# Cross attention with row turns one slot later, a spread prologue, and plain fp32 projections in the first layer

## The reference, cut to what matters

```python
x = cross_attn(layernorm(x, ln2_g, ln2_b), context, q2_w, k2_w, v2_w, o2_w, o2_b) + x
...
q = linear(x, qw).reshape(Bq, Nq, H, DH)
k = linear(ctx, kw).reshape(Bq, Nk, H, DH)
v = linear(ctx, vw).reshape(Bq, Nk, H, DH)
sim = jnp.einsum('bihd,bjhd->bhij', q, k) * scale
attn = jax.nn.softmax(sim, axis=-1)
out = jnp.einsum('bhij,bjhd->bihd', attn, v).reshape(Bq, Nq, D)
return linear(out, ow, ob)
```

## Time and profile before

| | |
|---|---|
| median of three runs | 4440.8 us (4432.99 to 4448.74) |
| the profiled execution | 4438.94 us, its span 4437.1 us |
| mean granted clock of TensorE | 0.935 of full |
| busy over the span: TensorE, VectorE, ScalarE, POOL | 90%, 68%, 41%, 41% |
| narrow cross attention | first DMA at 1042.66, first score 1091.37, next stage 1414.97 |
| wide cross attention | first DMA at 3607.91, first score 3626.93 |

### The profile page before, as it was taken

The page is one execution under the profiler, slowest core; times in us unless marked ns, Lnnn a source line. Parts: engine busy times, 40 slices in busy tenths (PEclk is TensorE's granted clock), DMA queues, the critical chain, the costliest instruction groups (busy, mean ns, idle before and its releaser), DMA issues. The chain is left out here.

```text
span 4437.1 us, 66504 instructions
## 1 busy us (share of the span) xinstructions
PE 4009.9 (90%) x25111; PEld 2704.9 (61%) x25111; DVE 3034.0 (68%) x4959; ACT 1797.1 (41%) x2646; POOL 1814.9 (41%) x1175
## 2 busy tenths in 40 slices
PE   0779999995877997998999999999999979999899
PEld 0633434432665776776666666666666647777687
DVE  6779999973776655776666766676666646656565
ACT  0227777773444333111333333333333333434332
POOL 0158800001333110001677877877787752212200
PEclk9869999996788998999999999999999978989999
DMA  4554534212342101777121211211112010000100
GB/s 120 169 87 72 62 38 49 35 18 54 59 72 48 43 11 33 268 277 271 49 72 49 71 50 49 72 49 60 61 49 72 25 38 1 10 10 1 35 15 20
DMA packets 311705, 293.29 MB, mean 66 GB/s; under 512 B 132684, under 2 KB 233612, under 8 KB 311140
## 3 DMA queue, kind: packets, MB, share of 16 engines
q1 hardware_dynamic: 309476, 282.53, 24.9%
q0 software_dynamic: 1920, 6.61, 0.5%
HBM read 160.74 MB, written 127.28 MB: 65 GB/s over the span
## 5 line engine op out<-in xcount | busy, mean ns | idle before, releaser
L1702 POOL TENSOR_TENSOR f_sums<-f_sums,f_probs 128x1024 f32<-128x1024 f32 x384 | 915.6, 2384 | 154.6 <-ACT f_probs L1821 116.9
L1719 DVE TENSOR_REDUCE f_mx<-f_s 128x1 f32<-128x512 f32 x1024 | 659.8, 686 | 374.9 <-PE f_s L1844 363.7
L1821 ACT ACTIVATE f_probs<-f_st 128x1024 f32<-128x1024 f32 x512 | 525.0, 1027 | 932.2 <-PE f_st L1867 927.4
L1331 DVE TENSOR_REDUCE f_mx<-f_s 128x1 f32<-128x512 f32 x1024 | 638.7, 683 | 50.0 <-PE f_s L1462 27.9
L1442 ACT ACTIVATE f_probs<-f_st 128x512 f32<-128x512 f32 x1024 | 536.0, 600 | 208.2 <-PE f_st L1479 207.8
L1844 PE MATMUL f_s<-f_k,f_q 64*128 64x512 f32 x3072 | 508.0, 409 | 20.4 <-DMA f_k<-k 13.5
L1867 PE MATMUL f_st<-f_q,f_k 64*128 64x512 f32 x3072 | 485.2, 390 | 1.1 <-ACT f_probs L1821 1.0
L1881 PE MATMUL f_acc<-f_probs,f_v 128*64 128x512 f32 x2048 | 466.5, 597 | 0.0
L1844 PEld LDWEIGHTS f_s<-f_k,f_q 64*128 64x128 f32 x3072 | 339.0, 186 | 163.9 <-issue 113.1
L2313 POOL TENSOR_TENSOR f_probs<-f_probs,f_rden 128x616 f32<-128x616 f32 x128 | 161.4, 1261 | 556.0 <-DVE f_rden L2379 556.0
L1867 PEld LDWEIGHTS f_st<-f_q,f_k 64*128 64x128 f32 x3072 | 366.3, 184 | 26.2 <-ACT f_probs L1821 3.8
(11 more groups left out here) (281 smaller groups left out, 8454.9 us busy)
## 6 DMA issues: line engine op xcount, KB each, us to landing
q<-f_stage SPq DMA_DIRECT2D x80, 512.0 KB, 2.9
k<-f_stage SPq DMA_DIRECT2D x80, 512.0 KB, 2.9
f_q<-q SPq DMA_DIRECT2D x32, 1024.0 KB, 5.1
f_k<-k SPq DMA_DIRECT2D x32, 1024.0 KB, 7.4
v<-f_v_stage SPq DMA_DIRECT2D x64, 256.0 KB, 3.1
f_v<-v SPq DMA_DIRECT2D x32, 512.0 KB, 8.5
f_q<-q SPq DMA_DIRECT2D x96, 128.0 KB, 4.3
f_k<-k SPq DMA_DIRECT2D x96, 128.0 KB, 7.0
```

What stands on the lines that cost most here:

```text
L1331: v.tensor_reduce(mx[:, i % 2, c:c + 1], bank[u % 4][:, :], AX_X, ALU.max).then_inc(s_free, 1)
L1702: g_.tensor_tensor(out, out, probs[:, n % NP, :, :], ALU.add).then_inc(sum_done, 1)
L1719: v.tensor_reduce(mx[:, i % 2, c:c + 1], bank[u % 3][:, :], AX_X, ALU.max).then_inc(s_free, 1)
L1821: a_.activation(probs[:, s % NP, :, :], stb[s % 2][:, :, :], ACT.Exp, scale=L.scale).then_inc(p_ready, 1)
```

## The change

- The turn. LEAD and TURN_AT are now (2, 5) narrow and (2, 4) wide. VectorE still makes xhat in n, but TensorE turns it in n+1, ScalarE scales it in n+2 and VectorE makes the low part in n+3 (wide only).
- The first layer's projections (narrow). h, wq, o and wo are plain fp32 tiles; a query is two products in place of six, a projection unit four in place of twelve. ht, low_rows, low_out and the weight splits are gone there.
- Two extra products. In the narrow form flip(n) first waits for t_done, then issues two products of the k tile, 128 columns by 512, into the flip's banks, and then waits for p_norm. Their results are overwritten by the flip.
- The prologue. Before the loop SP loads one context instead of all; in the narrow form the next ones go out behind stack(0), stack(1) and stack(2), in the wide form context(1) behind wo and the bias. The zeroing of their tiles is in POOL's loop at n = 1 to 3. wo has a buffer of its own (oraw); its split, in the wide form, is at n = 2 on ScalarE and n = 3 on POOL.
- POOL's bias add stands at slot 4 of a tile behind the division, instead of at slot 0 ahead of it.

```diff
@@ -2103,7 +2103,7 @@
-        LEAD, TURN_AT = (2, 5) if narrow else (1, 1)
+        LEAD, TURN_AT = 2, 5 if narrow else 4
@@ -2165,12 +2165,18 @@
-            ht = sb("ht", [P, DC, TT])
-            h = [[sb(f"h_{part}{k}", [P, DC, TT], F32R) for k in two] for part in ("hi", "lo")]
+            if narrow:
+                h = [[sb(f"h{k}", [P, DC, TT]) for k in two]]
+            else:
+                ht = sb("ht", [P, DC, TT])
+                h = [[sb(f"h_{part}{k}", [P, DC, TT], F32R) for k in two] for part in ("hi", "lo")]
...
+            wraw, oraw = sb("wraw", [P, DC * L.dim]), sb("oraw", [P, OCH * D])
+            if narrow:
+                wqr, wor = [wraw[:, :].rearrange("p (c n) -> p c n", c=DC)], [oraw[:, :].rearrange("p (c n) -> p c n", c=OCH)]
...
@@ -2183,11 +2189,12 @@
-            o = [sb("o_hi", [P, OCH, TT], F32R), sb("o_lo", [P, OCH, TT], F32R)]
+            o = [sb("o", [P, OCH, TT])] if narrow else [sb("o_hi", [P, OCH, TT], F32R), sb("o_lo", [P, OCH, TT], F32R)]
...
@@ -2229,22 +2235,19 @@
-                sp.dma_start(bias[:, :], bo.partition_broadcast(P)).then_inc(b_in, 16)
-                for bt in range(KVB):
-                    sp.wait_ge(zeroed, 2 * bt + 2)
-                    context(bt)
-                sp.wait_ge(w_lo, 1)
+                sp.wait_ge(zeroed, 2)
+                context(0)
...
@@ -2264,7 +2267,12 @@
                 if narrow:
                     for t in range(TILES):
                         stack(t)
+                        if t + 1 < KVB:
+                            sp.wait_ge(zeroed, 2 * t + 4)
+                            context(t + 1)
                 else:
+                    sp.wait_ge(zeroed, 4)
+                    context(1)
...
@@ -2285,33 +2293,33 @@
                 for n in range(FIRST, SLOTS):
...
-                    if p == 0:
-                        pool.wait_ge(n_["chain"], (t + 1) * self.STATS_STEPS)
-                        xt = x_sb[:, t * TB:(t + 1) * TB, :]
-                        g_.tensor_tensor(xt, xt, bias[:, :].unsqueeze(1).broadcast_to((P, TB, D)), ALU.add).then_inc(biased, 1)
...
+                    if 0 < n < KVB:
+                        zero(n)
+                    if n == 3 and not narrow:
+                        pool.wait_ge(w_hi, 2)
+                        lo, hi = (wor[x][:, :, :].rearrange("p c n -> p (c n)") for x in (1, 0))
+                        g_.tensor_tensor(lo, oraw[:, :], hi.bitcast(F32), ALU.subtract).then_inc(w_lo, 1)
+                    if p == 4:
+                        pool.wait_ge(b_in, 16)
+                        pool.wait_ge(n_["chain"], (t + 1) * self.STATS_STEPS)
+                        xt = x_sb[:, t * TB:(t + 1) * TB, :]
+                        g_.tensor_tensor(xt, xt, bias[:, :].unsqueeze(1).broadcast_to((P, TB, D)), ALU.add).then_inc(biased, 1)
@@ -2381,14 +2390,14 @@
-                    if acc_of(n - 3):
+                    if acc_of(n - 3) and not narrow:
                         low_out(*acc_of(n - 3))
...
-                    if turn_of(n - 2):
-                        low_rows(turn_of(n - 2))
+                    if turn_of(n - 3) and not narrow:
+                        low_rows(turn_of(n - 3))
@@ -2426,24 +2436,26 @@
-                    if turn_of(n - 1):
-                        scale(turn_of(n - 1))
+                    if turn_of(n - 2):
+                        scale(turn_of(n - 2))
@@ -2472,11 +2484,13 @@
-                    for j, (k, a, bb) in enumerate(self.H_PASSES):
+                    passes = [(k, 0, 0) for k in range(DC)] if narrow else self.H_PASSES
+                    for j, (k, a, bb) in enumerate(passes):
@@ -2506,9 +2520,13 @@
                 def flip(n):
-                    pe.wait_ge(p_norm, n + 1)
                     if n > 0:
                         pe.wait_ge(t_done, n)
+                    if narrow:
+                        busy = kt[0][0][:, :, :].rearrange("p j m -> p (j m)")
+                        for r in range(2):
+                            t_.matmul(tbk[:, r, :], busy[:, 0:P], busy[:, 0:512], start=True, stop=True)
+                    pe.wait_ge(p_norm, n + 1)
@@ -2529,20 +2547,26 @@
-                        work = [(c, x, w) for c in range(part * half, part * half + half) for x, w in ((0, 0), (0, 1), (1, 0))]
+                        work = [(c, x, w) for c in range(part * half, part * half + half) for x, w in (((0, 0),) if narrow else ((0, 0), (0, 1), (1, 0)))]
@@ -2556,8 +2580,8 @@
-                    if turn_of(n):
-                        turn(turn_of(n))
+                    if turn_of(n - 1):
+                        turn(turn_of(n - 1))
```

More of the change, by code:

```diff
@@ L2201, in cross_block @@
             KV = 16 * (6 + H // G if narrow else 3)
-            ZERO = KVB * 2
             WOL = 16 * (G if narrow else 1)
-            kind_sem = dict(tp=hh_done, q=q_lo, acc=o_lo, y=y_done)
+            kind_sem = dict(tp=hh_done, q=q_lo, acc=o_hi if narrow else o_lo, y=y_done)
             @block.sync
@@ L2287, in _ @@
                 self.norm_rstd(pool, n_, 0)
[L2288 to L2293, removed]
-                if narrow:
[L2295 to L2300, removed]
+                if narrow:
+                    g_.memset(oraw[:, :], 0.0).then_inc(o_zeroed, 1)
+                else:
+                    pool.wait_ge(w_hi, 1)
+                    lo, hi = (wqr[x][:, :, :].rearrange("p c n -> p (c n)") for x in (1, 0))
+                    g_.tensor_tensor(lo, wraw[:, :], hi.bitcast(F32), ALU.subtract).then_inc(w_lo, 1)
                 for n in range(FIRST, SLOTS):
@@ L2359, in _ @@
                 turn_rows(0)
-                low_rows(0)
+                if not narrow:
+                    low_rows(0)
                 for c in range(QCH if narrow else 2):
@@ L2399, in scale @@
                         act.wait_ge(r_ready, at["tp", t, c] + 1)
[L2400 to L2404, removed]
+                    if not narrow:
+                        if t > 0:
+                            act.wait_ge(hl_done, t)
+                        for c in range(DC):
+                            a_.activation(ht[:, c, :], bank[at["tp", t, c] % 4][:, :], ACT.Identity, bias=bet[:, c:c + 1],
+                                          scale=gam[:, c:c + 1]).then_inc(ht_done, 1)
                     if t >= 2:
@@ L2428, in _ @@
                 act.wait_ge(gb_in, 32)
[L2429 to L2430 removed]
+                if not narrow:
+                    act.wait_ge(w_in, 16)
+                    a_.activation(wqr[0][:, :, :].rearrange("p c n -> p (c n)"), wraw[:, :], ACT.Copy).then_inc(w_hi, 1)
                 scale(0)
@@ L2440, in _ @@
                         a_.activation(flat, flat, ACT.Exp, scale=L.scale).then_inc(p_exp, 1)
+                    if n == 2 and not narrow:
+                        act.wait_ge(wo_in, WOL)
+                        a_.activation(wor[0][:, :, :].rearrange("p c n -> p (c n)"), oraw[:, :], ACT.Copy).then_inc(w_hi, 1)
                     for key in q_of(n):
@@ L2474, in query @@
                     pe.wait_ge(hh_done, DC * (t + 1))
-                    pe.wait_ge(hl_done, t + 1)
+                    if not narrow:
+                        pe.wait_ge(hl_done, t + 1)
                     clear(u)
-                    for j, (k, a, bb) in enumerate(self.H_PASSES):
+                    passes = [(k, 0, 0) for k in range(DC)] if narrow else self.H_PASSES
+                    for j, (k, a, bb) in enumerate(passes):
                         ins = t_.matmul(bank[u % 4][:, :], wqr[a][:, k, c * P:(c + 1) * P], h[bb][t % 2][:, k, :],
-                                        start=j == 0, stop=j == len(self.H_PASSES) - 1)
+                                        start=j == 0, stop=j == len(passes) - 1)
                     ins.then_inc(r_ready, 1)
@@ L2531, in project @@
                     u, half = at["y", t, part, j], OCH // 2
-                    pe.wait_ge(o_lo, nth("acc", t, part * half + half - 1))
-                    pe.wait_ge(w_lo, 2)
+                    pe.wait_ge(kind_sem["acc"], nth("acc", t, part * half + half - 1))
+                    if narrow:
+                        pe.wait_ge(wo_in, WOL)
+                    else:
+                        pe.wait_ge(w_lo, 2)
                     clear(u)
@@ L2543, in _ @@
                 turn(0)
-                pe.wait_ge(w_hi, 1)
-                pe.wait_ge(w_lo, 1)
+                if narrow:
+                    pe.wait_ge(w_in, 16)
+                else:
+                    pe.wait_ge(w_hi, 1)
+                    pe.wait_ge(w_lo, 1)
                 for c in range(QCH if narrow else 2):
```

27 lines of the change are left out of this document (13 added, 14 removed).

## The result

The changed kernel takes 4382.37 us, the median of four runs (4365.83 to 4391.96), for 4436.9 before in the same comparison: a ratio of 0.987, 95% interval 0.985 to 0.9889. Timed once more, on the chip of the last experiments, it took 4380.48 for 4438.5, 0.9861 (0.9835 to 0.9887). So the change gives 54 to 58 us by the medians; the forecast was 75.

A forecast was written before the change was run, and what follows sets the result against it. TensorE was taken as the bound, idling for xhat before each turn with a slow clock behind. Narrow -25 and wide -50 us took the profiled 4438.9 to 4364, hence 4366 on 4440.8; range 4335 to 4402.

The forecast's parts named there:

- Step 1: Narrow stage: turning a slot later removes the 3.38 us wait for xhat; a turn adds 1.5 us, turning tiles -23.6 together.
- xhat ends 5.8 us after slot 5's score starts ... 1.9 xhat: Narrow turning tile: VectorE's xhat is done before TensorE finishes slots 5 and 6, about 6.0 us, so the wait goes.
- the forecast's own signs: Narrow tiles 33 to 37 us, clock over 0.95, no turn wait over 1 us; wide tiles 53 to 56 at 1.00.
- Step 2: Narrow projections: plain fp32 products cost +1.5 us a tile, at 0.44 a record; low_rows and low_out leave off the path.
- The lower bound there: Narrow plain products: -4 us a tile, if a record took 0.24 us as the reduced ones do.
- Step 3: Narrow flips: two extra products a slot add 3.8 us a tile, nothing hiding them; with plain products the seventh tile is +3.1.
- rival A: Narrow stage: clock still drops once a tile, some 5 us each, so the stage gives 0; whole 4391 us, chance 0.12.
- Step 4: Narrow prologue: first score 8.4 us earlier, second tile starts 4 earlier after a DMA wait and takes 39.0 for 40.8.
- Step 5: Wide stage: -50 us; five turning tiles -42 at 54.3 for 62.7, seventh -9.6, longer prologue +2.
- B: Narrow stage: low clock holds throughout, +21 us a tile, so the kernel is slower at 4559 us; chance 0.04.
- C: Wide stage gives half: waits for scale's banks or the longer prologue cost 25 us more; whole 4391 us, chance 0.09.
- D: Both stages: the turn was not the cause and tiles don't shorten; whole some 4440 to 4480 us, chance 0.03.

The follow-up runs named there:

- the second profile: The changed kernel run and profiled once more with no edit, on the same chip as the runs beside it: 4380.48 us, 0.9861.

## Why the prediction was right, and where it was off

By stage it said -25 and -50; the profile has -16 and -47.

- **Step 1, the narrow turn: the cause was right, its price was not.** The wait of 3.38 us went, the clock stays at 1.00, and putting the turn back costs 32 us. But four turning tiles gave 4 x (37.7 - 40.9) = -12.8 for the -23.6 forecast. The step that failed is "xhat ends 5.8 us after slot 5's score starts ... 1.9 xhat". The bias add was described as part of the change and then priced nowhere: it puts POOL's 2.41 us beside xhat, which grows to 3.95, and slots 5 and 6 take 9.3 us for about 7.5. With it out of the way a tile is 35.7 for the forecast's 35.0. By the forecast's own signs (tiles of 33 to 37 us, no wait of the turn over 1 us) 37.7 and the wait of 1.14 fall outside.
- **Step 2, plain products: right in size, wrong on what else goes.** These are a projection, the two queries and the extra products behind each, slots 0 and 1 of the seventh tile (timeline of TensorE, after):

```profile
1329.50 1.99 PE L2560 MATMUL f_r<-f_oraw,f_o 128*128 128x256 f32 x8
1331.15 0.82 PE L2528 MATMUL f_t<-f_ks 128*128 128x512 f32 x2
...
1333.34 3.70 PE L2492 MATMUL f_r<-f_h,f_wraw 128*128 128x512 f32 x8
1336.47 1.03 PE L2528 MATMUL f_t<-f_ks 128*128 128x512 f32 x2
```

  Two queries take 3.13 us (1333.34 to 1336.47), 0.39 a record for the 0.44 assumed; a projection 1.65 for 1.75. In the seventh tile the plain form costs 1.4 where 1.5 stood. (The lower bound there is -3.2 by the forecast's own figures, not -4; nothing came near it.) What the forecast set to the side, that low_rows and low_out leave "VectorE, off the path", was not off it: with them back a turning tile is 3.4 us longer, most of it at the low clock.
- **Step 3, the extra products: dear in the sum, and their use not seen.** Charged with 3.8 us less what idle time takes, they cost 2.5 in the seventh tile (34.3 less 30.4, less the 1.4 of the plain products) and 1.7 in a turning one. The seventh tile moved by +3.9 for +3.1. The sum treated them as cost alone. Without them rival A comes true, 38 to 41 us a tile, so the argument against A from the earlier trace rows held only for a TensorE that has them. Nor do they hold the clock by themselves: it falls with them too where the turn is put back (0.85 to 0.88) and where the projections are reduced (0.91 to 0.92).
- **Step 4, the narrow prologue.** The first score came 10.6 us earlier for 8.4, with the ninth score waiting 3.23 us for the stack's DMA as the queue of SP said; the second tile starts 6.4 us earlier for 4. It was then 42.0 us and not 39.0. With the bias add at slot 0 it is 38.3: slot 6 again, and slot 7 behind it, 6.2 us for 4.3, in which the clock falls (low from 1171.8 to 1175.2). The last tile and the tail gave -2.1 for +1.
- **Step 5, the wide stage.** Five tiles gave 267.4 for 313.7, -46 for -42, since the wait for scale's banks is 0.5 us and not 1.3; the seventh 52.2 for 61.6, as said. The prologue cost +5.0 and not +2, and the tail is 3.9 longer. The tail goes with the clock: 27.1 us where it is at full clock throughout, as before, 28.8 where it is low for 3.4 us (the second profile), 31.3 where it is low for 10.2 (the first). What lowers it there was not tried.
- **The rivals.** A is real but kept away by the extra products; B, C and D did not come. No narrow tile passed 44 us.

The stages give -63 together, 12 less than the forecast; the medians say -54 and -58, within the scatter of the rest. Taking the clash of xhat and POOL away gave 12 us in the narrow stage, as much as the stages lack. The other misses go both ways: narrow prologue -2.4, second tile +3.0, seventh +0.8, last tile and tail -3.1; wide prologue +3, five tiles -4, tail +3.9. That they nearly cancel is luck.

## What to carry to other kernels

When an instruction moves from one engine's slot to another, look at what the neighbour engine does at the new time, not only at its own queue: an add on GpSimd that nobody waits for held up a VectorE step that everyone waited for. A wait taken off the path has two parts, the idle time and the slow clock behind it, and the second can be the larger: in the wide stage the waits were 12.5 us of the 38 to 40 that the late turn is worth. Filler work can pay for itself by keeping the clock (10 us of the narrow stage with the long wait, 5 with the short one, in profiles; the medians don't separate either pair). When a step is moved in a pipeline, try the slots around it: a turn whose scale fell beside a projection made a slot of 12.5 us, and one slot up its longest was 8.5.

## What the runs showed of the hardware

- A VectorE tensor_scalar of 128x256 (0.40 us) that meets a GpSimd tensor_tensor stands still until that ends: 2.45 us beside an add of 2.41, 0.93 beside a division of 1.22, in both cases ending 0.15 us behind it. The maximum, the subtraction and the sum of the softmax (0.80, 0.80, 0.78 us) kept their times where they began beside the add (six, one and one of them in the run with the add at slot 0).
- Plain fp32 records of 512 columns start 0.39 us apart over all 128 rows, two to a product, for 0.23 to 0.24 of a reduced record; so one plain product costs 0.78 us for the 0.7 of the three reduced ones it replaces, and spares the other engines the splitting.
